# Cross attention in a four-layer perceiver: score matmuls on 64 of 128 rows of the array

## The chip, the core and the metric

The kernel runs on one core of a Trainium2 chip. A core has five engines with their own instruction streams: TensorE (PE; its weight loads are listed as PEld), VectorE (DVE), ScalarE (ACT), GpSimd (POOL) and SyncE (SP, which here issues transfers). They meet in semaphores alone. Matmuls read SBUF and write PSUM, which has eight banks of 512 f32 values on 128 partitions. The metric is the device time of one execution in microseconds. It is given as the median of several runs; the profile is of one more execution.

## What is computed

The reference is a model with four layers. Each has a cross attention to a context, a self attention and a feed-forward part. There are 32 batches of 32 tokens, 128 features, 16 heads of 8 features, and a context of 257 rows for each batch. All is f32. The change is in the cross attentions of layer 2 (with an additive score bias `fside`) and of layer 3 (without one):

```python
q = heads(x @ Wq.T); k = heads(ctx @ Wk.T); v = heads(ctx @ Wv.T)     # 16 heads of 8 features
scores = einsum('bhqd,bhkd->bhqk', q, k) / sqrt(8)  (+ bias[b, h, q, k] in layer 2)
attn = softmax(scores)
out = einsum('bhqk,bhkd->bhqd', attn, v) @ Wo.T
```

## The kernel before

The whole model is one program. In both cross attentions the order of work is written out by hand for each engine, with semaphores between them. The first four and the last four batches are unrolled; the 24 between them run in a hardware loop, four batches a pass on PE, DVE and ACT and two on POOL.

*The score trick.* Four heads form a head group, `HG` = 4 groups. POOL multiplies the 32 query columns of a batch with a mask (`mask16`, L2516) that keeps, for each head, only the eight feature rows of this head. The result `x_qb` has 512 columns, 32 for each head, so 128 for each group. A matmul with the 128 columns of group g as weights and `x_k` (128 features x 257 keys) as moving data gives the scores of four heads x 32 queries on 128 partitions, in PSUM bank 2 + g. All 128 feature rows take part in it, though outside the group's own 32 rows the weights are zero.

*One batch on PE* (`x_four`), where k is the batch and k-1 the one whose weights are now ready:

1. wait for the masked queries (`xqb`); `x_score` for groups 0 and 1
2. `x_turn(0)`: transposes of exp(scores) of batch k-1, groups 0 and 1, into bank 6 (L1047)
3. `x_keys`: the key projection of batch k+1 into bank 0 (L1020)
4. `x_turn(1)`: transposes of groups 2 and 3 into bank 7
5. `x_score` for groups 2 and 3
6. `x_values`: the value projection of batch k+1 (L1027)
7. `x_pv` of batch k-1: the sums (L1062) and the products with the values (L1067), both with 32 columns of the array for each group, so that group g lands on partitions 32g to 32g+31 of bank 1

*One batch on DVE*: the row maximum of groups 0 and 1 (layer 2: `tensor_tensor_reduce`, L2171 and L2173, which adds the bias and takes minus the maximum; layer 3: `tensor_reduce`, L2180); the copy of bank 7 to SBUF (`x_turned`, L2188); the maximum of groups 2 and 3; the copy of the values (`x_values`, L2194); then the tail of batch k-1 (L1650, L2206, L2208), which starts when `x_pv` is done. *ACT*: the copy of bank 6 (L1531), the copy of the keys, then four exponentials (through the helper at L1204), the second pair after the second maximum. *POOL*: after DVE's tail of batch k-1 the sums of the four heads (L2533, L2539, L2544) with the spreading of the exponentials' sums for batch k (L2527) between them, then the masked queries of batch k+2 (L2516). SP loads context and bias into four buffers in turn.

Waits on PE: in layer 2 the scores of a pair wait for the maximum of the same pair one batch before (`xmax`), in layer 3 groups 0 and 1 for the exponentials (`xexp`); `x_turn` waits for exponentials, `x_values` for the copied keys, `x_pv` for both copies of the transposes and for the spread sums.

Other lines named below: L651, products of weight matrices in the preparation of layer 1's attention, matmuls on 64 rows, first 8 with rows 0 to 63 and then 8 with rows 64 to 127, each into another bank for each half; L472, a 128-row matmul that follows them; L842 and L884, 128-row and 64-row matmuls of a self attention.

Of the kernel before, what the change touches and what calls it, by code (L numbers as in the profile page):

```python
# [20 lines left out]
P = 128  # L21
# [4 lines left out]
KEYS = 257  # L26
# [93 lines left out]
def perceiver(nc, ctxT, ctxN, fside, mask, wpack, wrows, l1x_w, units, relb, x_in, out):  # L120
    ctx = ExitStack()
    with ctx:
# [23 lines left out]
        PS = ctx.enter_context(nc.psum_tensor("PS", [P, 8, 512], F32))  # L146
# [19 lines left out]
        def ar(a, n):  # L166
            return AR[:, a:a + n]
# [48 lines left out]
        c_F = [c_buf(k, KPAD, HG * KEYS).rearrange("p (g k) -> p g k", g=HG) for k in range(4)]  # L216
# [17 lines left out]
        y_at = lambda h: 8 * (h % 2) + h // 2  # L234

        x_q = ar(0, TOK)
        x_qb = [ar(1024 + 512 * q, 512) for q in range(2)]
        x_k = [ar(2048 + 257 * q, 257) for q in range(2)]
        x_v = [ar(2564 + 256 * k, 256).rearrange("p (c n) -> p c n", c=2) for k in range(4)]
# [199 lines left out]
        def _(pe):  # L439
# [231 lines left out]
            for t in range(NT):  # L671
                if t % 4 == 0:
                    half_taken(t // 4)
                m = pe.matmul(PS[:, 6, 8 * t:8 * t + 8], XNT[:, P * t:P * t + P], w("l0f_gate"),
                              start=True, stop=True)
# [335 lines left out]
            def cross(kname, vname, biased, src, bias=None):  # L1011

                sel = w("head_mask")[:, 0:32]

                def x_keys(k, first=False):

                    pe.wait_ge(sig[f"ctx_landed{k}"], seen.up(f"ctx_landed{k}", 32 if biased else 16))
                    if not first:
                        pe.wait_ge(sig["xv_taken"], seen.up("xv_taken"))
                    pe.matmul(PS[:, 0, 0:KEYS], w(kname), c_T[k][:, 0:KEYS], start=True, stop=True)\  # L1020
                        .then_inc(sig["xk_ready"], 1)

                def x_values(k):

                    pe.wait_ge(sig["xk_taken"], seen.up("xk_taken"))
                    for c in range(2):
                        m = pe.matmul(PS[:, 0, P * c:P * c + P], c_T[k][:, P * c:P * c + P], w(vname),  # L1027
                                      start=True, stop=True)
                    m.then_inc(sig["xv_ready"], 1)

                def x_score(q, g, first):

                    if not first and biased and g % 2 == 0:
                        pe.wait_ge(sig["xmax"], seen.up("xmax"))
                    if not first and not biased and g < 2:
                        pe.wait_ge(sig["xexp"], seen.up("xexp"))
                    m = pe.matmul(PS[:, 2 + g, 0:KEYS], x_qb[q][:, P * g:P * g + P], x_k[q], start=True, stop=True)  # L1037
                    if g % 2:
                        m.then_inc(sig["xs_ready"], 1)

                def x_turn(q, pair, last=False):

                    if biased or last or pair:
                        pe.wait_ge(sig["xexp"], seen.up("xexp", 2))
                    for c in range(2):
                        for g in (2 * pair, 2 * pair + 1):
                            m = pe.transpose(PS[:, 6 + pair, 256 * c + P * (g % 2):256 * c + P * (g % 2) + P],  # L1047
                                             x_p[q][:, g, P * c:P * c + P], ident)
                    m.then_inc(sig["xpt_ready"], 1)

                def x_pv(k, first=False, last=False):

                    q = k % 2
                    if last:
                        pe.wait_ge(sig["xv_taken"], seen.up("xv_taken"))
                    pe.wait_ge(sig["xsum_spread"], seen.up("xsum_spread", 2))
                    pe.wait_ge(sig["xpt_a"], seen.up("xpt_a"))
                    pe.wait_ge(sig["xpt_d"], seen.up("xpt_d"))
                    if not first:
                        pe.wait_ge(sig["xt_ready"], seen.up("xt_ready", 3))  # L1060
                    for g in range(HG):
                        pe.matmul(PS[32 * g:32 * g + 32, 1, 384:448], sel,  # L1062
                                  x_m[q][:, g, :, :].rearrange("p a f -> p (a f)"), start=True, stop=True,
                                  skip_group_check=True)
                    for c in range(2):
                        for g in range(HG):
                            m = pe.matmul(PS[32 * g:32 * g + 32, 1, 256:384], x_v[k][:, c, 32 * g:32 * g + 32],  # L1067
                                          x_pt[:, c, P * g:P * g + P], start=(c == 0), stop=(c == 1),
                                          skip_group_check=True)
                    m.then_inc(sig["xu_ready"], 1)  # L1070

                def x_four(first=False, last=False):
                    for k in range(4):
                        q, start, end = k % 2, first and k == 0, last and k == 3
                        pe.wait_ge(sig["xqb"], seen.up("xqb"))
                        x_score(q, 0, start)
                        x_score(q, 1, start)
                        if not start:
                            x_turn(1 - q, 0)
                        if not end:  # L1080
                            x_keys((k + 1) % 4)
                        if not start:
                            x_turn(1 - q, 1)
                        x_score(q, 2, start)
                        x_score(q, 3, start)
                        if not end:
                            x_values((k + 1) % 4)
                        if not start:
                            x_pv((k - 1) % 4, first and k == 1)

                if biased:
                    pe.wait_ge(sig["rows_landed"], 16)
                    for k, name in enumerate(("l2x_g1", "l2x_be1")):
                        pe.transpose(PS[:, 7, P + P * k:2 * P + P * k], row(name), ident)
                pe.matmul(PS[:, 7, 0:32], w(vname), c_lastT, start=True, stop=True).then_inc(sig["vlast_ready"], 1)
                x_keys(0, True)
                x_values(0)
                pe.wait_ge(sig["vlast_taken"], seen.up("vlast_taken"))
                x_four(first=True)
                seen.loop(B // 4 - 2, {f"ctx_landed{k}": 32 if biased else 16 for k in range(4)} |  # L1100
                          ({"xmax": 8} if biased else {}) |
                          {"xexp": 16, "xsum_spread": 8, "xt_ready": 12} |
                          {k: 4 for k in "xk_taken xv_taken xqb xpt_a xpt_d".split()}, lambda i: x_four())
                x_four(last=True)
                x_turn(1, 0, last=True)
                x_turn(1, 1, last=True)
                x_pv(3, last=True)
                seen.up("xt_ready", 3)
                seen.up("xmax", 2 if biased else 2 * B)
                if bias:  # L1110
                    pe.wait_ge(sig["bias_ready"], bias)
                carry(src)
                pe.wait_ge(sig["x_out"], seen.up("x_out", B if biased else B + 1))
# [532 lines left out]
        def _(dve):  # L1646
# [507 lines left out]
            def cross(biased, bv):  # L2154
# [9 lines left out]
                def x_max(k, pair):  # L2164

                    q = k % 2
                    dve.wait_ge(sig["xs_ready"], seen.up("xs_ready"))
                    if biased:
                        if pair == 0:
                            dve.wait_ge(sig[f"ctx_landed{k}"], seen.up(f"ctx_landed{k}", 32))  # L2170
                        dve.memset(SM[:, 502:503], 0.0)  # L2171
                        for g in (2 * pair, 2 * pair + 1):
                            ins = dve.tensor_tensor_reduce(  # L2173
                                out=x_s[q][:, g, :], in0=PS[:, 2 + g, 0:KEYS], in1=c_F[k][:, g, :], scale=-1.0,
                                scalar=3.0e38, op0=ALU.add, op1=ALU.min, accum_out=x_neg[q][:, g:g + 1])
                            name = "xmax" if g % 2 else "dve_ran"
                            ins.then_inc(sig[name], 1)
                            seen.up(name)
                    else:
                        dve.tensor_reduce(x_neg[q][:, 2 * pair:2 * pair + 2],  # L2180
                                          PS[:, 2 + 2 * pair:4 + 2 * pair, 0:KEYS], AX, ALU.max, negate=True)\
                            .then_inc(sig["xmax"], 1)
                        seen.up("xmax")
                    dve.wait_ge(sig["xmax"], seen.up("xmax", 0))
# [612 lines left out]
```

## Time and profile before

| | us |
|---|---|
| median of 3 runs | 1305.49 (1302.21 to 1307.1) |
| the profiled execution | 1307.56 |
| its span | 1305.8 |

| engine | busy us | share of the span | instructions |
|---|---|---|---|
| PE | 1174.5 | 90% | 10141 |
| PEld | 852.2 | 65% | 10141 |
| DVE | 692.9 | 53% | 2019 |
| ACT | 611.8 | 47% | 1286 |
| POOL | 379.9 | 29% | 551 |

The mean granted TensorE clock over the span is 0.937 of full speed. The cross attention of layer 2 takes about 542 to 687 us of the span, that of layer 3 about 1085 to 1227 us. Busy time counts an instruction from its start to its modelled end. Matmuls are pipelined, so that a record lasts longer than the distance to the next, and the distance of the starts says how fast they follow each other. Idle time in square brackets stands before an instruction, with the instruction that ended it; idle time under 0.15 us isn't listed.

### The profile page before, as it was taken

What the parts mean: (1) busy time and instruction counts of PE and PEld (TensorE: products, weight loads), DVE (VectorE), ACT (ScalarE), POOL (GpSimd) and SP (SyncE); (2) the same over time, 40 slices, a digit from 0 to 9 for tenths busy, and PEclk for the clock granted to TensorE, in tenths of its full rate; (3) what the DMA queues carried; (4) which work ended last, traced back from release to release, by engine and by line L of the source; (5) the groups of instructions that cost most, each with busy time, mean ns of one, the idle gap of its engine ahead of it and who ended that gap; (6) DMA issues with size and microseconds to landing.
All of it is one profiled execution on the core that took longest, in us unless ns stands there. A gap on an engine that the chain in (4) does not pass through costs nothing.

```text
span 1305.8 us, 29423 instructions
## 1 busy us (share of the span) xinstructions
PE 1174.5 (90%) x10141; PEld 852.2 (65%) x10141; DVE 692.9 (53%) x2019; ACT 611.8 (47%) x1286; POOL 379.9 (29%) x551
## 2 busy tenths in 40 slices
PE   5786999999999799899998367899999999999798
PEld 2343665688787565688875155577777767888575
DVE  2267445555555453677774253534333346777653
ACT  2153223434333543577774232434343436777654
POOL 2014300221121024255550060123140504555450
PEclk8597999999999988999999759999999999999979
DMA  9610012122222000355430301011112110111000
GB/s 286 171 65 1 25 36 66 40 53 51 59 52 55 2 2 29 119 150 154 141 106 1 42 9 43 13 49 50 60 49 61 49 53 22 33 29 35 23 4 17
DMA packets 71018, 75.23 MB, mean 58 GB/s; under 512 B 6288, under 2 KB 63712, under 8 KB 70552
## 3 DMA queue, kind: packets, MB, share of 16 engines
q1 hardware_dynamic: 67880, 66.18, 18.7%
q0 software_dynamic: 1152, 6.97, 1.5%
q10 hardware_dynamic: 1904, 0.98, 0.5%
q8 instruction: 53, 0.87, 0.3%
q14 instruction: 29, 0.24, 0.1%
HBM read 71.49 MB, written 0.52 MB: 55 GB/s over the span
## 4 chain that ended last, share of the span: by engine, by line
PE 78%; DVE 6%; ACT 5%; DMA 5%; issue 2%; POOL 1%; ACTq 1%; SPq 1%; DVEq 0%; POOLq 0%
PE PS L503 13%; PE PS L515 13%; PE PS L1037 9%; PE PS L740 4%; PE PS L1047 4%; PE PS L704 4%; DMA CTX<-in_ctxT 3%; PE PS L747 2%; PE PS L506 2%; PE PS L691 2%; PE PS L823 2%; PE PS L1020 2%; PE PS L1067 2%; PE PS L1027 2%; ACT AR L1204 1%
## 5 line engine op out<-in xcount | busy, mean ns | idle before, releaser
L515 PEld LDWEIGHTS PS<-WB,AR 128*128 128x128 f32 x1568 | 189.2, 192 | 43.1 <-issue 38.6
L515 PE MATMUL PS<-WB,AR 128*128 128x128 f32 x1568 | 189.6, 275 | 0.0
L1204 ACT ACTIVATE AR<-PS,WB 128x512 f32<-128x512 f32 x160 | 110.0, 687 | 151.6 <-PE PS L503 145.5
L1037 PE MATMUL PS<-AR 128*128 128x257 f32 x512 | 138.5, 393 | 2.7 <-POOL AR L2516 2.7
L1775 DVE SCALAR_TENSOR_TENSOR ACC<-PS,SM,ACC 128x128 f32<-128x128 f32 x192 | 54.0, 344 | 95.6 <-PE PS L515 94.6
L1037 PEld LDWEIGHTS PS<-AR 128*128 128x128 f32 x512 | 87.1, 190 | 22.6 <-issue 8.4
L1650 DVE TENSOR_TENSOR AR<-PS,AR 128x512 f32<-128x512 f32 (+2 forms) x71 | 49.7, 701 | 97.4 <-ACT AR L1204 39.8
L503 PE MATMUL PS<-ZT,WB 128*128 128x512 f32 x208 | 101.3, 610 | 0.0
L503 PE MATMUL PS<-XNT,WB 128*128 128x512 f32 x168 | 87.5, 627 | 4.9 <-DVE AR L1650 3.4
L1204 ACT ACTIVATE AR<-PS 128x512 f32<-128x512 f32 (+2 forms) x82 | 43.5, 530 | 103.3 <-PE PS L506 76.6
L1204 ACT ACTIVATE AR<-PS,SM 128x257 f32<-128x257 f32 x136 | 64.6, 475 | 41.6 <-DVE SM L1858 32.0
L2460 POOL TENSOR_TENSOR AR<-AR,SM 128x516 f32<-128x516 f32 x32 | 33.7, 1054 | 155.6 <-ACT SM L1204 93.8
L1047 PE MATMUL PS<-W,AR 128*128 128x128 f32 x512 | 76.8, 273 | 1.5 <-ACT AR L1204 1.4
L1775 DVE SCALAR_TENSOR_TENSOR X<-PS,SM,X 128x128 f32<-128x128 f32 x168 | 47.2, 343 | 56.7 <-PE PS L515 56.4
L1047 PEld LDWEIGHTS PS<-W,AR 128*128 128x128 f32 x512 | 63.5, 141 | 15.2 <-ACT AR L1204 2.6
L1204 ACT ACTIVATE AR<-AR,SM 128x257 f32<-128x257 f32 x128 | 65.3, 510 | 15.4 <-DVE SM L2173 10.3
L2516 POOL TENSOR_TENSOR AR<-AR,W 128x512 f32<-128x512 f32 x64 | 67.0, 1048 | 18.1 <-POOL OT L2544 13.1
L740 PE MATMUL PS<-CTX,AR 128*128 128x129 f32 x512 | 62.4, 275 | 0.0
L1204 ACT ACTIVATE AR<-AR 128x1024 f32<-128x1024 f32 (+1 forms) x57 | 50.0, 877 | 24.8 <-DVE AR L1979 13.8
L704 PE MATMUL PS<-AR,CTX 128*128 128x512 f32 x128 | 60.4, 594 | 0.8 <-ACT AR L1364 0.8
L2495 POOL TENSOR_TENSOR ACCB<-RB,SM 128x1024 f32<-128x1024 f32 x5 | 9.6, 1911 | 176.8 <-DVE SM L1650 176.8
L740 PEld LDWEIGHTS PS<-CTX,AR 128*128 128x128 f32 x512 | 59.8, 191 | 0.5 <-issue 0.5
(295 smaller groups left out, 2227.8 us busy)
## 6 DMA issues: line engine op xcount, KB each, us to landing
WB<-in_units SPq DMA_DIRECT2D x49, 385.0 KB, 3.1
CTX<-in_fside SPq DMA_DIRECT2D x32, 514.0 KB, 4.0
CTX<-in_ctxT SPq DMA_DIRECT2D x96, 130.0 KB, 2.1
CTX<-in_ctxT SPq DMA_DIRECT2D x8, 520.0 KB, 5.2
CTX<-in_ctxN SPq DMA_DIRECT2D x16, 258.0 KB
CTX<-in_ctxN SPq DMA_DIRECT2D x32, 129.0 KB, 2.3
AR<-in_ctxN SPq DMA_DIRECT2D x32, 64.5 KB, 3.0
AR<-in_l1x_w POOLq DMA_DIRECT2D x1, 2048.0 KB, 9.8
```

Source lines behind the costliest of these rows:

```text
L503: m = pe.matmul(bank(2 * c), WB[:, q, 128 * c:128 * c + 128], src[:, 512 * hh:512 * hh + 512], start=True, stop=True)
L506: m = pe.matmul(bank(2 * c + 1), WB[:, q, UNIT + 128 * c:UNIT + 128 * c + 128], src[:, 512 * hh:512 * hh + 512], start=True, stop=True)
L515: m = pe.matmul(PS[:, 4 + hh, 128 * t:128 * t + 128], f_h[hh][:, c, 128 * t:128 * t + 128], WB[:, q, 2 * UNIT + 128 * c:2 * UNIT + 128 * c ...
L704: m = pe.matmul(bank(1 + c), c_T[k][:, P * c:P * c + P], rhs, start=True, stop=True)
L740: m = pe.matmul(o, y_P[q][:, c, P * g:P * g + P], c_N[k][:, c, :], start=(c == 0), stop=(c == 1))
L1037: m = pe.matmul(PS[:, 2 + g, 0:KEYS], x_qb[q][:, P * g:P * g + P], x_k[q], start=True, stop=True)
L1047: m = pe.transpose(PS[:, 6 + pair, 256 * c + P * (g % 2):256 * c + P * (g % 2) + P], x_p[q][:, g, P * c:P * c + P], ident)
L1204: return act.activation(o, i, fn, **k)
L1650: return dve.tensor_tensor(o, a, b, op)
L1775: ins = dve.scalar_tensor_tensor(out=a, in0=y, scalar=f_w[:, 4 * hh + t, bass.ds(e, 1)], in1=a, op0=ALU.mult, op1=ALU.add)
L2460: pool.tensor_tensor(y_T[k % 2], y_last[k].unsqueeze(1).broadcast_to([P, HG, FQ]), y_pl[:, :, k].unsqueeze(2).broadcast_to([P, HG, FQ]), A ...
L2516: pool.tensor_tensor(x_qb[q].rearrange("p (h q) -> p h q", h=H), qv, m16, ALU.mult)\
```

## The change

The score matmul of a group reads only the 64 feature rows that hold its head group: rows 0 to 63 for head groups 0 and 1, rows 64 to 127 for 2 and 3. So that the two matmuls of a pair lie in different halves, the head groups are dealt out anew: position g works on head group `x_group[g]`, with `x_group = (0, 2, 1, 3)`. Positions 0 and 1 hold head groups 0 and 2, positions 2 and 3 hold 1 and 3. Banks, buffers, the order of the instructions, their count and the semaphores stay with the position. Where head groups matter by number, the slice follows: the bias in DVE's reduction, the value columns, and the output partitions of `x_pv`.

```diff
         x_q = ar(0, TOK)
+        x_group = (0, 2, 1, 3)
@@ x_score
-                    m = pe.matmul(PS[:, 2 + g, 0:KEYS], x_qb[q][:, P * g:P * g + P], x_k[q], start=True, stop=True)
+                    r = slice(64 * (g % 2), 64 * (g % 2) + 64)
+                    own = x_group[g]
+                    m = pe.matmul(PS[:, 2 + g, 0:KEYS], x_qb[q][r, P * own:P * own + P], x_k[q][r],
+                                  start=True, stop=True)
@@ x_pv
                     for g in range(HG):
-                        pe.matmul(PS[32 * g:32 * g + 32, 1, 384:448], sel,
+                        own = 32 * x_group[g]
+                        pe.matmul(PS[own:own + 32, 1, 384:448], sel,
                                   x_m[q][:, g, :, :].rearrange("p a f -> p (a f)"), start=True, stop=True,
                                   skip_group_check=True)
                     for c in range(2):
                         for g in range(HG):
-                            m = pe.matmul(PS[32 * g:32 * g + 32, 1, 256:384], x_v[k][:, c, 32 * g:32 * g + 32],
+                            own = 32 * x_group[g]
+                            m = pe.matmul(PS[own:own + 32, 1, 256:384], x_v[k][:, c, own:own + 32],
                                           x_pt[:, c, P * g:P * g + P], start=(c == 0), stop=(c == 1),
                                           skip_group_check=True)
@@ x_max on DVE, layer 2
-                                out=x_s[q][:, g, :], in0=PS[:, 2 + g, 0:KEYS], in1=c_F[k][:, g, :], scale=-1.0,
+                                out=x_s[q][:, g, :], in0=PS[:, 2 + g, 0:KEYS], in1=c_F[k][:, x_group[g], :], scale=-1.0,
```

## Rows read from the trace of the kernel before

**Rows 1.** The page: chain that ended last by engine, and the score line's group.

```profile
PE 78%; DVE 6%; ACT 5%; DMA 5%; issue 2%; POOL 1%; ACTq 1%; SPq 1%; DVEq 0%; POOLq 0%
...
L1037 PE MATMUL PS<-AR 128*128 128x257 f32 x512 | 138.5, 393 | 2.7 <-POOL AR L2516 2.7
```

**Rows 2.** Windows: one loop pass (four batches) of layer 2, one of layer 3.

```profile
core 0: us, PE busy (x) PEld busy (x) DVE busy (x) ACT busy (x) POOL busy (x), PEclk, DMA share, GB/s
621.18:639.10 17.92, 17.64 (x184) 14.77 (x184) 14.24 (x61) 13.53 (x41) 10.04 (x24) 1.00 0.53 147
1149.29:1166.78 17.49, 17.49 (x189) 14.76 (x185) 13.22 (x29) 13.29 (x41) 10.03 (x24) 1.00 0.11 30
```

**Rows 3.** Timeline of PE, one batch of layer 3: start, us, engine, line, operation.

```profile
1149.29 1.13 PE L1037 MATMUL PS<-AR 128*128 128x257 f32 x4
1150.26 0.60 PE L1047 MATMUL PS<-W,AR 128*128 128x128 f32 x4
...
1151.57 1.03 PE L1037 MATMUL PS<-AR 128*128 128x257 f32 x4
1152.44 0.61 PE L1027 MATMUL PS<-W,CTX 128*128 128x128 f32 x4
1152.97 0.32 PE L1062 MATMUL PS<-AR,W 128*32 128x64 f32 x8
```

**Rows 4.** Timelines of PE: into and out of the 64-row form.

```profile
787.05 0.66 PE L842 MATMUL PS<-W,AR 128*128 128x128 f32 x4 [1.06 <-ACT AR L1204]
787.63 1.16 PE L884 MATMUL PS<-SM,ACCB 64*128 64x128 f32 x8
...
92.71 1.98 PE L472 MATMUL PS<-X,W 128*128 128x512 f32 x4
```

**Rows 5.** L651 on PE: its first burst, and a window on that burst's start.

```profile
89.29 3.50 PE L651 MATMUL PS<-AR 64*128 64x128 f32 x32
...
89.28:90.72 1.44, 1.43 (x12) 1.43 (x13) 1.00 0.00 0
```

**Rows 6.** Timeline of DVE, layer 3: the copy of the transposes, four batches.

```profile
1151.84 0.69 DVE L2188 COPY AR<-PS 128x512 f32<-128x512 f32 x1 [0.52 <-PE PS L1047]
...
1156.14 0.69 DVE L2188 COPY AR<-PS 128x512 f32<-128x512 f32 x1 [0.17 <-PE PS L1047]
...
1160.58 0.69 DVE L2188 COPY AR<-PS 128x512 f32<-128x512 f32 x1 [0.41 <-PE PS L1047]
...
1164.95 0.69 DVE L2188 COPY AR<-PS 128x512 f32<-128x512 f32 x1 [0.43 <-PE PS L1047]
```

**Rows 7.** Timelines: masked queries on POOL and scores on PE, layers 3 and 2.

```profile
1156.67 1.05 POOL L2516 TENSOR_TENSOR AR<-AR,W 128x512 f32<-128x512 f32 x1 [0.27 <-POOL OT L2544]
1158.03 1.13 PE L1037 MATMUL PS<-AR 128*128 128x257 f32 x4
1161.17 1.05 POOL L2516 TENSOR_TENSOR AR<-AR,W 128x512 f32<-128x512 f32 x1 [0.27 <-POOL OT L2544]
...
637.93 1.05 POOL L2516 TENSOR_TENSOR AR<-AR,W 128x512 f32<-128x512 f32 x1 [0.28 <-PE PS L1037]
639.11 1.13 PE L1037 MATMUL PS<-AR 128*128 128x257 f32 x4 [0.24 <-POOL AR L2516]
```

**Rows 8.** Timelines of DVE and PE in the loop of layer 2.

```profile
628.11 0.69 DVE L2188 COPY AR<-PS 128x512 f32<-128x512 f32 x1
631.85 0.06 DVE L2171 MEMSET SM<- 128x1 f32 x1 [0.55 <-DVE AR L2208]
632.21 1.03 PE L1037 MATMUL PS<-AR 128*128 128x257 f32 x4
633.64 0.06 DVE L2171 MEMSET SM<- 128x1 f32 x1 [0.15 <-DVE AR L2188]
```

**Rows 9.** Timeline of DVE: first two batches of layer 2 with that copy.

```profile
547.62 0.69 DVE L2188 COPY AR<-PS 128x512 f32<-128x512 f32 x1 [0.85 <-PE PS L1047]
...
551.99 0.69 DVE L2188 COPY AR<-PS 128x512 f32<-128x512 f32 x1 [0.47 <-PE PS L1047]
```

## The prediction

> **What bounds the kernel now.** I read the page's chain first: TensorE (PE) carries 78% of the path that ended last, and line 1037, the score matmul, is its largest line outside the feed-forward layers, with 138.5 us of busy time for 512 records [rows 1]. The program has 64 batches with 4 such matmuls each, so every f32 matmul is two records, A1 and A2 below for the first of a pair, B1 and B2 for the second. An average says nothing of the limit, so I took one pass of each cross attention's loop (four batches) next. Layer 3 needs 17.49 us with PE busy for all of it, 4.37 us a batch. Layer 2 runs the same PE program, but needs 17.92 us with PE busy for 17.64 [rows 2]. The granted clock is 1.00 in both, the level of 2.4 GHz. So PE is the bound in layer 3, and in layer 2 something else already is.
>
> In layer 2 it is VectorE (DVE). Busy for 14.24 of 17.92 us, it looks idle a fifth of the time, but the idle pieces are its own: 0.55 us at the loop's turn, and 0.15 us before the memset at 633.64, although the score matmuls that it could be waiting for ended at 633.24. The copy of the turned weights, where it could wait for PE, starts without a listed idle time [rows 8]. I count no wait for PE over 0.03 us there. DVE's program is serial with small gaps and takes the 17.92 us by itself; PE does the waiting. In layer 3 DVE idles before the same copy for 0.52, 0.17, 0.41 and 0.43 us, for PE's transposes [rows 6].
>
> **The change part by part.** *The matmuls.* A pair of score matmuls takes 0.87 us (1151.57 to 1152.44) [rows 3], four records at 0.217. Each new one uses 64 rows of the array, a pair uses both halves and two PSUM banks. Moved columns and records stay as they are, so one matmul alone is no shorter: what counts is whether the halves run side by side. The nearest rows are L651, 64-row matmuls, 16 in the lower half and then 16 in the upper (records). Twelve fit into 1.44 us, so 0.111 us each after 0.11 us for the first weights. 32 of them, one after the other, would put the last start at 89.29 + 0.11 + 31 x 0.111 = 92.84. The row ends at 92.79 and a record lasts 0.27, so it started at 92.52 [rows 5]: 0.32 us, three records, went beside others at the one place where the half changes. The upper half began while three records of the lower half had still to start or run. In a pair exactly that is asked for: B1's weights must pass A1's matmul and A2's weights and matmul. I take full overlap: 0.434 + 0.007 for the pair, a saving of 0.43. Bounds: 0 if nothing overlaps, 0.22 if only B1 beside A2.
>
> The Trainium skill, "TensorE: Matmul & The Clock Gate", Part 3 (The mechanism), says that only weight loads are pulled ahead while matmuls start and end strictly in program order; the order here is A1 A2 B1 B2, so by it only B1 runs beside A2. Rows 5 speak for more, since under that rule one record would have been saved and not three. Its result is the second rival.
>
> *The switches.* Whenever PE changes the tile form it loses time at two places. Before the first 128x32 form, 1152.44 to 1152.97 is 0.53 us for four records that take 0.44 otherwise: 0.10 us to run empty. After it, the first pair takes 0.97 and not 0.87 (1149.29 to 1150.26): 0.10 us for weights that nothing hides [rows 3]. The 64-row form pays the same both ways: from L651's last start at 92.52 to L472 at 92.71 are 0.19 where 0.11 is the distance, and L842's last start (787.05 + 0.66 - 0.27 = 787.44) to L884 are 0.19 [rows 4]; the uncovered weights come on top. So 0.20 us a switch. A batch runs, on PE: pair 0 and 1, transposes, keys, transposes, pair 2 and 3, values, then the 128x32 products. It has two switches now, around the products. With the change the pair behind the products enters from them, at the price already paid; leaving it is new, and so are entering and leaving the second pair: three more, 0.60 us. Bounds: 0 and 0.60 a batch.
>
> PE per batch: 4.37 - 2 x 0.43 + 0.60 = 4.12 us. First pair with its exit: -0.23, second pair with both switches: -0.03.
>
> *Relabelling.* Groups 1 and 2 change places in the bias slice of the DVE reduction, in the value slice and in the output rows. The same operations with the same sizes: nothing, and no wait or DMA is added. The later semaphore of a pair comes with B2 in either order.
>
> *What is late next, layer 3.* DVE without its waits for PE: 17.49 - (0.52 + 0.41 + 0.43 - 3 x 0.15) = 16.6, or 4.15 a batch. The longest loop goes over two batches: DVE's copy (1151.84), reduction, values, tail, GpSimd's sums and masked queries (1156.67 to 1157.72), the scores at 1158.03, transposes, copy again at 1160.58 [rows 6, 7]. Of PE's saving only the first pair lies in it: 0.23 in two batches. Its slack is what lies between the end of the masked queries and the scores beyond the 0.12 us that such a wait costs (layer 2, 637.93 + 1.05 = 638.98 to about 639.10, where PE did wait). The distances over four batches are 0.30, 0.31, 0.19 and 0.21 us (the queries that end at 1157.72 and at 1162.22 are shown; the scores follow at 1158.03 and one batch later) [rows 7]. Four batches are two rounds of the loop, which have 0.18 + 0.07 over. Four batches: 17.49 - 0.46 - 0.25 = 16.8, or 4.20 each. 24 batches lie in loops: 24 x 0.17 = 4.1. The eight unrolled ones have more slack and follow PE: about 0.43 for the very first pair, 6 x 0.25 for the rest: 1.9. Layer 3: 6.0 us. Bounds of the loop part: 24 x 0.06 = 1.4 (slack alone) and 24 x 0.25 = 6.
>
> *Layer 2.* The loop's 24 batches belong to DVE: 0. In the unrolled ones DVE does wait for PE's transposes, 0.85 us at the first batch, 0.47 at 551.99 [rows 9] and as much at three more. I take 0.43 for the first pair and 4 x 0.25 for the others: 1.4. Bounds: 0 and, if part of DVE's gaps of 0.15 were PE's after all, 24 x 0.15 = 3.6 more.
>
> **Sum.** 6.0 + 1.4 = 7.4 us, and 0.1 for DVE's waits of up to 0.03 us in layer 2: 7.5. The profiled execution took 1307.56 us, a span of 1305.8 and 1.8 around it; it becomes 1300.1. Against the median of the runs, 1305.49, it is 1298.0.
>
> **The rivals.**
> 1. *Layer 3 barely moves* (0.18): the loop through DVE and GpSimd has less slack than I read and gives 1.4 in place of 4.1, or a second loop through ScalarE holds it. For it: DVE's own 4.15 is close. 1305.5 - 1.4 - 1.9 - 1.4 = 1300.8; with the unrolled parts halved 1302.5.
> 2. *Half overlap, slower* (0.12): B1 can run only beside A2. A pair takes 0.65, PE 4.37 - 0.44 + 0.60 = 4.54 a batch. Layer 3: 32 x 0.17 = 5.4. Layer 2 passes DVE's 4.48: 24 x 0.06 + 8 x 0.17 = 2.8. Together 1313.7. It decides as soon as a pair saves under 0.30 us, half of the 0.60 of the switches. Against it: three records saved and not one [rows 5]. For it: 257 columns and a fresh form have no row.
> 3. *No overlap* (0.05): the change then doesn't do what it says; PE at 4.97. 32 x 0.60 + 24 x 0.49 + 8 x 0.60 = 35.8: 1341.
> 4. *More than forecast* (0.13): switches cheaper, or layer 2 gains too; 3.6 there and 2 in layer 3: 1292.4.
>
> **How the numbers follow.** My forecast has 0.52, 1298.0, with 1296 to 1300 as its own range. A measurement of this kernel can tell about 0.5% from no change, 6.5 us, so the line is 1299.0 and runs through my forecast: of its 0.52 I count 0.34 below it. Faster: 0.34 + 0.13 = 0.47; same: 0.18 + 0.18 = 0.36; slower: 0.12 + 0.05 = 0.17. For 8 in 10, the range takes in rivals 1 and 4 with the free end of the switches, and some of the way to rival 2: 1291.5 to 1307. Rivals 2 and 3, 0.17, stay outside.
>
> **What would show it.** In the changed profile L1037 has the form 64x128, and a pair starts its four records within about 0.22 us. If they start 0.217 apart, rival 3; 0.65 us for a pair, rival 2. From a pair to the next form are 0.20 us. Four batches of layer 3 take 16.8 us with PE no longer busy for all, and a new wait on L2516 before L1037; 16.5 or 17.2 would be rivals 4 and 1. Four batches of layer 2 still take 17.9; if they fall under 17.6, my reading of DVE was wrong. A granted clock below 1.00 in either would upset all of it.

## The result, and the profile after

The changed kernel takes 1296.16 us, the median of 10 runs (1287.62 to 1301.09), where the kernel before took 1305.35 us beside it (10 runs, 1299.25 to 1313.37). The ratio is 0.9925, with a 95% interval of 0.9895 to 0.9954: faster by 0.75%, or some 9 us. The profiled execution took 1298.77 us with a span of 1297.0, which is 8.8 us under the span of before, at a mean granted clock of 0.935 (before: 0.937).

The page of the changed kernel, chain of work that ended last, and the score line's group (it was L1037 and is L1040; in all of the new kernel's rows lines have moved by one to six):

```profile
PE 65%; issue 9%; DVE 7%; POOL 7%; ACT 5%; DMA 4%; POOLq 1%; ACTq 1%; SPq 1%; DVEq 0%
...
L1040 PE MATMUL PS<-AR 64*128 64x257 f32 x512 | 92.4, 428 | 6.5 <-POOL AR L2522 5.9
```

Against [rows 1] the score line is busy for 92.4 us and not 138.5, though each record lasts longer (428 and not 393 ns): records run side by side. PE holds 65% of the chain and not 78%; POOL went from 1% to 7%, and the scores now wait 5.9 us for the masked queries and not 2.7.

The same two windows as [rows 2], one loop pass (four batches) of layer 2 and one of layer 3; columns are length, busy time and instructions of PE, PEld, DVE, ACT and POOL, granted clock, DMA share, GB/s:

```profile
612.79:630.53 17.74, 16.60 (x186) 11.23 (x186) 14.25 (x61) 13.53 (x41) 10.06 (x24) 1.00 0.51 151
1145.90:1162.79 16.89, 16.66 (x185) 11.51 (x186) 13.25 (x29) 13.33 (x41) 10.04 (x24) 1.00 0.11 32
```

Layer 3 went from 17.49 to 16.89 us a pass, layer 2 from 17.92 to 17.74. DVE, ACT and POOL do the same work in both; PE has idle time of its own in both now, 1.14 us in layer 2 and 0.23 in layer 3.

One batch of layer 3 on PE, to be held against [rows 3]:

```profile
1155.71 0.81 PE L1040 MATMUL PS<-AR 64*128 64x257 f32 x4 [0.17 <-POOL AR L2522]
1156.45 0.66 PE L1051 MATMUL PS<-W,AR 128*128 128x128 f32 x4
...
1157.91 0.70 PE L1040 MATMUL PS<-AR 64*128 64x257 f32 x4
1158.54 0.71 PE L1028 MATMUL PS<-W,CTX 128*128 128x128 f32 x4
```

The second pair (1157.91) and its exit take 0.63 us to the start of the values at 1158.54, where they took 0.87 before. The pair that waited for the queries (1155.71) takes 0.74 to the transposes and not 0.97.

Where the 8.8 us lie can be read from the starts of the products' last matmuls in the records, one for each of a layer's 32 batches; the step from one to the next is a batch. The products of batch 3 are the first that the loop makes, so two of the 31 steps lie ahead of the loop, 24 in it and five behind it. Layer 2 gave 3.37 us (0.38 from the first scores to the first products, 0.64 in the first two steps, 1.38 in the loop, 0.97 in the last five), layer 3 gave 5.68 (0.09, 0.63, 3.69 and 1.27). Together 9.05; the rest of the program differs by 0.26 the other way.

### The profile page after: what moved, and what is told of

Its sections match the earlier page's. It is cut to its first block, busy times and chain, and to the rows that moved or that the text cites. A ratio compares the mean times of both kernels' runs of the same rounds, so it can differ in the third digit from the quotient of the medians.

```text
span 1297.0 us, 29423 instructions
## 1 busy us (share of the span) xinstructions
PE 1161.0 (90%) x10141; PEld 798.1 (62%) x10141; DVE 692.3 (53%) x2019; ACT 612.3 (47%) x1286; POOL 380.5 (29%) x551
## 4 chain that ended last, share of the span: by engine, by line
PE 65%; issue 9%; DVE 7%; POOL 7%; ACT 5%; DMA 4%; POOLq 1%; ACTq 1%; SPq 1%; DVEq 0%
PE PS L504 13%; PE PS L516 13%; PE PS L741 4%; PE PS L705 4%; POOL AR L2522 4%; DMA CTX<-in_ctxT 2%; PE PS L748 2%; PE PS L507 2%; PE PS L1040 2%; PE PS L692 2%; PE PS L824 2%; PE PS L1051 2%; ACT XN L1210 1%; PE PS L452 1%; PE PS L843 1%
## 5 line engine op out<-in xcount | busy, mean ns | idle before, releaser
L1040 PE MATMUL PS<-AR 64*128 64x257 f32 x512 | 92.4, 428 | 6.5 <-POOL AR L2522 5.9
L1051 PE MATMUL PS<-W,AR 128*128 128x128 f32 x512 | 80.3, 280 | 1.1 <-ACT AR L1210 0.9
L1051 PEld LDWEIGHTS PS<-W,AR 128*128 128x128 f32 x512 | 58.4, 141 | 29.1 <-issue 12.7
L1040 PEld LDWEIGHTS PS<-AR 64*128 64x128 f32 x512 | 40.7, 184 | 32.4 <-issue 13.9
```

The source lines that it names most:

```text
L1040: m = pe.matmul(PS[:, 2 + g, 0:KEYS], x_qb[q][r, P * own:P * own + P], x_k[q][r], start=True, stop=True)
```

## The experiments

There are ten runs: eight kernels ran once each, and then the changed kernel and one of the eight were timed (last part of this section). "Pass" is always four batches in a loop, taken from the records. The kernel before took 1306.23 us beside the kernels with one half, layer 3 alone, one wait, and queries first, and 1304.78 beside the other four. The whole times of single runs differ by several us from the clock elsewhere in the program (last section), so the passes carry the verdicts.

### Is it the overlap?

The pair's two matmuls keep the 64-row form, but both lie in the same half: positions 0 and 1 hold head groups 0 and 1.

```diff
-        x_group = (0, 2, 1, 3)
+        x_group = (0, 1, 2, 3)
-                    r = slice(64 * (g % 2), 64 * (g % 2) + 64)
+                    r = slice(64 * (g // 2), 64 * (g // 2) + 64)
```

> Head groups are paired 0 with 1 and 2 with 3 again, so that the two 64-row matmuls of a pair lie in the same half of the array. All forms and switches stay as in the changed kernel, only the overlap is gone. My theory (the gain is the overlap, the switches are its price): a pair takes 0.87 us in place of 0.44, PE needs 4.05 + 2 x 0.43 = 4.9 us a batch in both layers, four batches 19.6 to 19.7 us; that is 32 x 0.55 us more than before in layer 3, and in layer 2 24 x 0.44 + 8 x 0.55: about 1338 us. Rival (the 64-row form is cheaper in itself, for instance in its weight loads): a pair stays well under 0.87 and the time within 10 us of before.

It took 1340.31 us; both passes 19.63. The second pair in PE's timeline of layer 3, and the window of the pass:

```profile
1184.26 1.13 PE L1040 MATMUL PS<-AR 64*128 64x257 f32 x4
1185.32 0.71 PE L1028 MATMUL PS<-W,CTX 128*128 128x128 f32 x4
```

```profile
1181.54:1201.17 19.63, 19.63 (x195) 14.14 (x185) 13.24 (x29) 13.31 (x41) 10.04 (x24) 1.00 0.11 27
```

The pair with its exit takes 1.06 us and PE is busy for the whole pass, 4.91 us a batch. Against the 4.37 of before that is 0.54 for three more switches. From first to last products layer 2 takes 150.30 us and layer 3 150.07, where they took 137.05 and 134.19. So the form alone costs 29.1 us there (34 between the whole times, which differ elsewhere too), and the overlap of the halves brings back that and 8.6 more. The time of this kernel lies close to rival 3 of the prediction (no overlap, 1341). In part that is luck, since the rival was worked out with 0.60 for the switches and 0.54 was measured.

### Is each layer's gain its own?

Layer 2 keeps all 128 rows; layer 3 is changed.

```diff
-                    r = slice(64 * (g % 2), 64 * (g % 2) + 64)
+                    r = slice(0, P) if biased else slice(64 * (g % 2), 64 * (g % 2) + 64)
```

> 64-row score matmuls in layer 3 alone; layer 2 keeps 128 rows (with the groups dealt out anew in both). My theory, from the two traces: layer 3 as in the changed kernel, four batches in the loop 16.89 us; layer 2 back to 17.92 us and 3.4 us longer than in the changed kernel: about 5.7 us under before. Rival (the time came from elsewhere, a clock window or the start): layer 2 keeps its 17.74 us, or layer 3 loses its gain.

1303.39 us. Layer 2's pass is back at 17.92 and layer 3's is 16.89; from the first products to the last, layer 2 takes 137.12 us (before 137.05) and layer 3 128.63 (after 128.60). The gains add up and neither layer touches the other. Since layer 2 deals out its groups anew here too, the dealing alone costs nothing. The whole time is 2.8 us under the run of before and not 5.7. That run has no trace, so how the 2.8 divide isn't shown. Against the profiled execution of before, the stretch between the layers is 5.7 us longer (411.7 us here, 405.9 in before and after) and the part ahead of layer 2's first products is 4.6 us shorter (544.66 and 549.24), though the work in both is the same.

### What holds layer 3: the queries from GpSimd, or waits inside the pair?

The masked queries and the scores that use them, in the changed kernel, layer 3 and then layer 2:

```profile
1154.54 1.05 POOL L2522 TENSOR_TENSOR AR<-AR,W 128x512 f32<-128x512 f32 x1 [0.27 <-POOL OT L2550]
...
618.87 0.70 PE L1040 MATMUL PS<-AR 64*128 64x257 f32 x4 [0.24 <-POOL AR L2522]
```

In layer 3 the queries end at 1155.59 and the scores (shown above) start 0.12 us later, at 1155.71; PE stands still for them in every second batch. The steps of a pass are 4.10, 4.39, 4.08 and 4.33 us. PE's own batch is 4.06 (the unrolled ones show it), so the other two are also 0.02 to 0.04 too long, and in the records the first pair is not as tight as the second: the weights of its second matmul start 0.04 to 0.12 us after those of its first, where the second pair has 0.006. In layer 3 each matmul of the first pair has a wait for an exponential of its own.

The first edit takes the two waits together into one, ahead of the first matmul:

```diff
-                    if not first and not biased and g < 2:
-                        pe.wait_ge(sig["xexp"], seen.up("xexp"))
+                    if not first and not biased and g == 0:
+                        pe.wait_ge(sig["xexp"], seen.up("xexp", 2))
```

> Changed kernel, and in layer 3 PE waits for both exponentials ahead of the first score matmul, in place of one wait ahead of each of the two. My theory: the wait of its own is what lets the second half start 0.11 us after the first in layer 3's first pair (its second pair starts 0.007 apart). Without it the first pair starts within 0.01 us, a batch without a wait for POOL falls from 4.166 to 4.055 us, and the loop over two batches gets 0.11 shorter: four batches 16.67 in place of 16.89, 2 us over the layer. Rival (the exponential itself comes late): the first matmul starts 0.1 later instead, nothing is gained.

The second edit lets GpSimd make the next queries ahead of the tail's sums, which wait for DVE:

```diff
                 def step(b, q, more=True):
-                    x_tail(b - 1, 1 - q, q)
                     if more:
                         x_queries(b + 2, q, False)
+                    x_tail(b - 1, 1 - q, q)
```

> Changed kernel, and POOL makes the masked queries of batch b+2 ahead of the tail of batch b-1 and not behind it, so that they no longer wait for DVE's tail. My theory (the loop over DVE's tail and POOL binds layer 3): PE's waits for the queries are gone there, every batch takes the 4.166 us of those that don't wait now, four batches 16.67 in place of 16.89, 1.5 to 2 us over the layer; layer 2 stays at 17.74 us for four, as DVE takes them by itself, although PE's waits there vanish too or move to another place. Rival 1 (DVE or ACT binds layer 3): 16.89 stays. Rival 2 (POOL binds layer 2 too): layer 2 falls by 0.1 us a batch or more.

One wait: pass 16.74, steps 4.06, 4.39, 4.06 and 4.25. The pair's second half is now at most 0.012 us late, but the steps with a wait for the queries stay long, so that 0.14 us are gained where 0.22 were expected. Queries first: pass 16.28, steps 4.06, 4.06, 4.06 and 4.11, where 16.67 was expected. The latter's windows (layer 2, layer 3), then the first pair in PE's timeline of layer 3:

```profile
611.20:628.94 17.74, 16.56 (x195) 11.21 (x184) 14.24 (x61) 13.52 (x40) 10.05 (x25) 1.00 0.51 149
1148.98:1165.26 16.28, 16.28 (x195) 11.27 (x185) 13.25 (x29) 13.32 (x41) 10.05 (x25) 1.00 0.12 33
```

```profile
1149.18 0.70 PE L1040 MATMUL PS<-AR 64*128 64x257 f32 x4
1149.82 0.66 PE L1051 MATMUL PS<-W,AR 128*128 128x128 f32 x4
```

Both edits together:

> Changed kernel with the queries made first and the single wait ahead of layer 3's first pair. The queries alone gave 16.28 us for four batches of layer 3, with most first pairs starting 0.007 us apart already, as PE's sequencer was no longer held. Theory: PE's own 4 x 4.055 = 16.22 binds and the wait adds at most the one late start in four batches (0.06 us): 16.22 to 16.28. Rival (the wait costs by itself): 16.0.

The pass is 16.30, and layer 2's 17.73. Beside the earlier queries the single wait brings nothing. In three batches of four a step is 4.06 with two waits as with one, so there the second wait has no price. At the turn of the loop the step is 4.14 with one wait and 4.11 with two, since the whole pair now starts 0.08 late and not its second half alone. The whole time was 1288.72.

### What did layer 2 gain from?

The prediction left the loop of layer 2 at 17.92. This is the group of DVE's copy of the transposes over the whole layer (542 to 700 us), first in the kernel before, then in the changed one; the last column is all idle time before it, and how much of that is put down to PE:

```profile
L2188 DVE COPY AR<-PS 128x512 f32<-128x512 f32 x32 | 22.1, 691 | 6.4 <-PE PS L1047 3.9
```

```profile
L2194 DVE COPY AR<-PS 128x512 f32<-128x512 f32 x32 | 22.1, 692 | 4.8 <-PE PS L1051 3.4
```

Idle time went from 6.4 to 4.8 us. Of the 1.6, 0.5 are in the part that has a releaser; 1.1 are in pieces too short to be listed. In the records of one pass those pieces are 0.116, 0.133, 0.122 and 0.035 us in before, and 0.035, 0.034, 0.034 and 0.123 in after. One piece of 0.12 stays, at the turn of the loop; two others shrink to 0.035. That is 0.18 us less, all that the pass lost. If these were waits for PE, then anything that puts PE ahead must take them away, the old score matmuls or not. So the kernel before, with GpSimd's queries first:

> The kernel before (128-row scores) with the masked queries made ahead of the tail on POOL. My theory: layer 3 was bound by PE alone, so four batches keep 17.49 us; in layer 2 PE no longer waits for POOL, runs a little ahead, and DVE loses the 0.18 us in four batches that it waited for the transposes: 17.92 becomes 17.74, about 1 us in all. Rival (POOL's loop held both layers before already): layer 3 falls under 17.4.

Layer 2's pass is 17.73 and layer 3's 17.49, and the four pieces are 0.035, 0.035, 0.034 and 0.122 here too. The 0.18 us were waits for PE, and 17.74 is what is left when they are gone, whichever edit does it.

What is the limit at 17.74? The next kernel has the queries first, and in layer 2 DVE copies only half of the value columns (128 of 256), so the products of layer 2 are made from half of the new values.

```diff
-                    dve.tensor_copy(x_v[k], PS[:, 0, 0:256].rearrange("p (c n) -> p c n", c=2))\
-                        .then_inc(sig["xv_taken"], 1)
+                    if biased:
+                        dve.tensor_copy(x_v[k][:, 0, :], PS[:, 0, 0:P]).then_inc(sig["xv_taken"], 1)
+                    else:
+                        ...
```

> Changed kernel with the queries first, and in layer 2 DVE copies only the first 128 of the 256 value columns, so the second half of the values there is old data; everything else is computed. A DVE copy of 512 columns takes 0.69 us and one of 256 takes 0.42, so 128 fewer take about 0.13 us less. Theory (DVE's serial program binds layer 2): four batches of layer 2 fall from 17.75 by 4 x 0.13 to 17.2 us, layer 3 keeps 16.28. Rival (ACT, PE or the loads bind layer 2): it stays over 17.6.

1286.11 us. Layer 2, the copy in DVE's timeline and the window of the pass:

```profile
606.75 0.29 DVE L2201 COPY AR<-PS 128x128 f32<-128x128 f32 x1
```

```profile
606.38:623.58 17.20, 16.57 (x196) 11.22 (x185) 13.71 (x61) 13.52 (x40) 10.04 (x25) 1.00 0.54 153
```

A copy takes 0.29 and not 0.42 us, 0.13 less; four of them are 0.53, and the pass is 0.54 shorter. What is taken from DVE comes off the pass. The windows say the same: the pass less DVE's busy time is 3.68 us before, 3.49 in the changed kernel and 3.49 here, and in the records of the latter two every idle piece stands behind an instruction of DVE's own. DVE's serial program is the limit of layer 2.

The opposite test makes PE faster there. Queries first, and in layer 2 the second pair right behind the first, so that two switches go:

```diff
                         x_score(q, 1, start)
+                        if biased:
+                            x_score(q, 2, start)
+                            x_score(q, 3, start)
```

> Changed kernel with the queries first, and in layer 2 the second pair of scores stands right behind the first, so that two of the five switches of the array's form are gone: PE's own time falls by 0.35 us a batch to 3.7. Theory (PE doesn't bind layer 2): four batches of layer 2 keep 17.75 us within 0.05. Rival (PE still binds in part): they fall by up to 1.4 us. It may also get slower, if DVE's copy has to wait for transposes that now come later.

PE's timeline in layer 2, and the window of a pass:

```profile
611.13 1.14 PE L1040 MATMUL PS<-AR 64*128 64x257 f32 x8
612.20 0.66 PE L1051 MATMUL PS<-W,AR 128*128 128x128 f32 x4
...
614.07 0.71 PE L1028 MATMUL PS<-W,CTX 128*128 128x128 f32 x4 [0.35 <-ACT AR L1214]
```

```profile
610.92:628.70 17.78, 15.95 (x196) 11.57 (x185) 14.25 (x61) 13.52 (x40) 10.03 (x25) 1.00 0.53 149
```

Eight records of two pairs take 1.07 us with their exit, and PE is busy for 15.95 us of the pass and not 16.56. The pass is 17.78 all the same. PE is not the limit. The layer as a whole is slower (135.67 us from first to last products against 133.97): in its unrolled batches the transposes now come behind four score matmuls and not two, and a step is 4.34 instead of 4.06 us. 1296.12 us in all.

### Is queries first worth having?

The changed kernel with GpSimd's queries first, and the changed kernel as it is, both timed on one chip beside the kernel before:

> The changed kernel with the queries first once more, now timed. By the layers' spans of its first look it is 9.3 us shorter than before in layer 3 and 3.1 in layer 2 (and what the first pair of each saves): 12.5 to 13 us under before, a ratio of 0.990. Rival: the order of the queries costs elsewhere, ratio 0.993 or more.

> The changed kernel itself, on the same chip: 9 us under before by the spans of its layers (3.0 + 5.6 + what the first pairs save), a ratio of 0.993; e9 lies 3.5 to 4 us under it.

Before: 1306.94 (23 runs). The change: 1300.01 (12 runs), ratio 0.995, interval 0.9922 to 0.9978. The change with the queries first: 1293.57 (12 runs), ratio 0.991, interval 0.9881 to 0.9939. The passes are 17.75 and 16.87 for the one, 17.75 and 16.28 for the other. From first to last products layer 3 took 124.87 us against 128.54, so 3.7 us are shown by the traces; the medians are 6.4 apart, and for the rest no cause is shown but the spread of single runs, 13 to 16 us within each of the two. Each of the two is faster than the kernel before, and by the traces queries first is the better of them.

## Why the prediction was right, and where it was not

The forecast was 1298.0 us against a median of 1305.49, a gain of 7.5; measured is 9.2 between medians (1305.35 and 1296.16), and 8.8 between spans. The sign, the mechanism and the wait that comes next held. That the whole time came within 1.8 us of the forecast is partly luck: the interval of the ratio leaves 6 to 14 us, and the later medians of the same two kernels are 6.9 apart. The terms can be held against the traces, one by one:

- *Full overlap of a pair.* Held. In the records of the pair at 1157.91 the matmuls start at 1157.909, 1157.916, 1158.230 and 1158.237: 0.32 us from first to last where three records of 0.217 were 0.65, and the next form's weights start 0.305 after the last. That the 0.007 belongs to the second matmul of the pair, and not to the second record of the first, can be read off where both matmuls have a wait. With the queries first the two weight loads that carry one start 0.007 apart, ahead of the two that don't; in the kernel with one half they are the first and third to start. Even where the second half is late, at 1155.71, its first matmul record (1155.826) starts ahead of the first half's second (1156.030). [Rows 5] were the right rows to choose. The Trainium skill, "TensorE: Matmul & The Clock Gate", Part 3 (The mechanism), has matmuls start strictly in program order; here B1 starts ahead of A2, so the measurement decides against it, and with it against rival 2 (1313.7), which was built on it. A pair alone shows this for records only, since the first of its two matmuls still starts and ends first. The records of [rows 5] show it for whole matmuls: the upper half's first one starts at 90.735, the lower half's last one, which the program has ahead of it, at 90.953. My sign for this was put too tightly: I said four starts within 0.22 us, and it is 0.33, since A2 starts a whole record plus uncovered weights behind A1.
- *Switches at 0.20 us.* Held within 0.05. Into the pair it is 0.20: 0.09 from the last transpose at 1157.707 to the weights at 1157.908 beyond the 0.11 that transposes are apart, and 0.10 for weights that nothing hides inside the pair (0.321 between a matmul's two records, where 0.217 is one). Out to the values it is 0.195, again in two halves. Out to the transposes it is 0.15, since their weights leave 0.06 uncovered and not 0.11. That is why PE's batch is 4.06 and not 4.12. The kernel with one half gives the three together: 0.54 where I had 0.60. The Trainium skill, "TensorEngine Tiling (Array Packing)", Key Properties, says that a change of mode drains TensorE. The trace agrees with about 0.09 us of it; the page gives no time.
- *Relabelling at nothing.* Held: DVE, ACT and POOL are busy for the same times within 0.04 us in both windows, and layer 2 with the dealing alone needs 17.92 us a pass as before.
- *Layer 3's loop.* 3.69 us where I had 4.1. The pass is 16.88 and I said 16.8. The limit is the loop that I named, DVE's tail, GpSimd's sums and queries, scores, transposes, copy: the wait on the queries came where I put it, and the pass falls to PE's 16.28 when it is taken out. What the sum had not is the late start of the second half behind a held wait (0.04 to 0.12 us a batch). By the kernel with one wait it is worth 0.14 of the pass.
- *DVE's own 4.15 us as the floor of layer 3.* Wrong, and it cost nothing only because the other loop was longer: with the queries first layer 3 runs at 4.07 a batch. I had subtracted the listed idle pieces before the copy and left 0.17 and 0.15 us pieces in; part of those was a wait for PE too. It is the same mistake as in layer 2.
- *Layer 3's unrolled batches.* 1.99 where I had 1.9, but otherwise divided, so the agreement is luck in part: the stretch up to the first products gave 0.09, where I had 0.43 for the very first pair, and the seven steps gave 0.27 each on average. Part of the reason is in the records of both kernels: the second score matmul of the second batch starts 0.51 us after the first, behind its wait for an exponential, so there is no overlap there to pay for the switches.
- *Layer 2's loop at 0.1.* Wrong: 1.38 us, of which 0.50 in the first pass and 0.17 to 0.18 in each of the other five. This is the step that failed. I wrote that I count no wait for PE over 0.03 us, because the copy of the transposes had no listed idle time. A piece under 0.15 us is not listed. Three of four batches had one of 0.12 to 0.13, and in two of them 0.08 and 0.10 of it were a wait for PE. The bound that I kept for it, 3.6 us, held. DVE as the limit is right all the same (the half copy), at 17.74 and not at 17.92.
- *Layer 2's unrolled batches at 1.4.* 1.99 us. I counted the first pair and four steps at 0.25. The first two steps went to PE's 4.06 (0.32 each), and the last five gave 0.97.

So the error of 1.5 us is layer 2's loop (1.3 too little) and its unrolled steps (0.6 too little), less layer 3's 0.3. Rival 4, "more than forecast", had this cause in part (3.6 in layer 2); rival 1 had none of it. The forecast itself lay only 1.0 us on the faster side of the 0.5% line; the 1.5 us come from two small terms of layer 2 that I had put too low, and are less than single runs differ by.

## What to carry to other kernels

A matmul whose weights are zero in half of the rows took no less time here when it was cut to 64 rows. It paid only when its neighbour sat in the other half; in all kernels here the neighbour also came directly behind it and wrote another bank, and what these two are worth wasn't tried. Count the changes of form first: three more per batch ate 0.54 of the 0.85 us that the overlap saved. When an engine looks like the limit although it has idle pieces, read its group's total idle time beside what is put down to a releaser: a remainder of 0.1 us for each instruction can hide a wait on somebody (here 0.08 and 0.10 in two batches of four, while another piece of 0.12 stayed in every kernel). And after PE has become faster, look at what another engine does just ahead of what PE needs: here the order of two steps on GpSimd was worth another 3.7 us.

## What the runs showed of the hardware

- Two f32 matmuls of 257 columns, each of two records, run side by side in the two 64-row halves, the second starting 0.007 us after the first and ahead of the first's second record. The pair takes 0.64 us with its exit, 1.06 in one half.
- With a wait between the two matmuls of such a pair the second still starts 0.007 us after the first in three batches of four when the queries are early. It starts 0.02 to 0.12 us after it in the changed kernel's loop, where PE's sequencer had just waited for the queries, and 0.06 to 0.08 at the turn of the loop when they are early.
- The granted clock is not the same from run to run at one place. The start of layer 3, from the first scores to the first products, in the changed kernel's first profile and in that of its later run:

```profile
1081.16:1087.70 6.54, 6.54 (x39) 4.04 (x39) 3.59 (x6) 4.65 (x14) 2.75 (x4) 1.00 0.08 22
```

```profile
1084.71:1093.80 9.09, 9.09 (x41) 5.67 (x44) 3.73 (x6) 4.93 (x15) 2.75 (x4) 0.62 0.06 16
```

The same program needs 2.55 us more here, with a granted clock of 0.62 in place of 1.00, so part of the stretch was at 1.2 GHz. The pairs of scores show it: 1.23 us in place of 0.70.

```profile
1086.12 1.23 PE L1040 MATMUL PS<-AR 64*128 64x257 f32 x4
```

In both, PE stood still for 0.76 us just before the first scores. The two runs of the kernel with the queries first were at the lower clock at this place as well (9.01 and 9.02 us); the kernel before (6.61) and the one with both edits (6.62) were not. What decides between the two levels here stays open. Over the whole stretch between the layers, from the last products of layer 2 to the first of layer 3, the two runs of the changed kernel differ by 8.1 us, again with the clock and with the same busy times of DVE and ACT:

```profile
682.32:1088.16 405.84, 352.92 (x2777) 245.64 (x2766) 167.38 (x553) 162.61 (x268) 96.21 (x57) 0.92 0.15 39
```

```profile
680.29:1094.20 413.91, 362.27 (x2777) 251.83 (x2766) 167.43 (x553) 162.58 (x268) 96.11 (x57) 0.90 0.15 38
```

The work there is the same in all kernels of this study. So single runs can differ by as much as the change is worth, and the whole time of the kernel with layer 3 alone (411.69 us in this stretch, 405.95 in before) says nothing to within 3 us about what its layer 3 is worth; the layer's own 128.63 us do.
